# Work moved in front of a branch between two attention paths, and a row load issued one block ahead

## The reference, cut to what matters

```python
support = (inputs @ weight).reshape(-1, H, D).transpose(1, 0, 2)      # H = 4 heads, D = 64
f1 = einsum('hnd,hd->hn', support, weight_u)[:, None, :]              # s_j, by source node
f2 = einsum('hnd,hd->hn', support, weight_v)[:, :, None]              # s_i, by target node
masked = leaky_relu(f1 + f2, 0.2) * adj_mat
m = max over the row where masked != 0
e = where(mask, exp(masked - m), 0)
out = (e / e.sum(axis=2)) @ support + bias + inputs @ proj_w.T + proj_b
```

## Time and profile before

| | |
|---|---|
| median of 3 runs | 1848.31 us (1845.47, 1851.26, 1848.31) |
| profiled execution | 1845.97 us, span 1844.2 us |
| mean granted TensorE clock | 0.963 |
| TensorE busy | 1675.1 us, 91% of the span |
| VectorE busy | 929.3 us, 50% |
| ScalarE busy | 955.2 us, 52% |
| chain that ended last | TensorE 51%, VectorE 4%, DMA 2%, ScalarE 2%, issue 2% |

### The profile page before, as it was taken

One profiled execution on the slowest core, in us unless ns is written; L12 is line 12 of the kernel. 1 busy time (PEld: TensorE's weight loads), 2 busy tenths in 40 slices (PEclk: granted clock), 3 DMA queues, 4 the chain that ended last, 5 costly groups with the idle time before them and its releaser, 6 DMA issues.

```text
span 1844.2 us, 41619 instructions
## 1 busy us (share of the span) xinstructions
PE 1675.1 (91%) x13344; PEld 1547.9 (84%) x13345; DVE 929.3 (50%) x2185; ACT 955.2 (52%) x2192; POOL 350.6 (19%) x315
## 2 busy tenths in 40 slices
PE   4799999999799994767989989989988999999998
PEld 3588888778799994657989979989987999999997
DVE  4578877888322222338877868867773111111111
ACT  1143443543434432347989979979834443443443
POOL 2110000000266663210000000000001333333332
PEclk9899999999899997788999999999998999999999
DMA  9990000005388886200000000000094666666664
GB/s 159 107 164 10 9 9 17 29 18 200 114 208 206 207 212 174 80 14 7 17 15 13 14 13 18 9 18 18 3 332 157 178 189 174 179 190 173 181 187 94
DMA packets 85581, 189.95 MB, mean 103 GB/s; under 512 B 13209, under 2 KB 59545, under 8 KB 76665
## 3 DMA queue, kind: packets, MB, share of 16 engines
q1 hardware_dynamic: 51801, 138.33, 22.9%
q0 software_dynamic: 31504, 48.97, 16.7%
q10 hardware_dynamic: 2192, 1.58, 0.3%
HBM read 188.98 MB, written 33.11 MB: 120 GB/s over the span
## 4 chain that ended last, share of the span: by engine, by line
PE 51%; DVE 4%; DMA 2%; ACT 2%; issue 2%; ACTq 0%; DVEq 0%; POOL 0%; SPq 0%; POOLq 0%
PE bank L1625 23%; PE bank L2107 12%; PE bank L2146 11%; PE bank L619 1%; PE bank L616 1%; DMA arena<-proj_b 1%; ACT arena L1376 1%; PE bank L2114 1%; DMA arena<-qd 1%; DVE arena L1469 0%; DVE arena L1471 0%; PE bank L2036 0%; PE bank L2010 0%; PE bank L606 0%; DVE arena L1413 0%
## 5 line engine op out<-in xcount | busy, mean ns | idle before, releaser
L1625 PE MATMUL bank<-arena 128*128 128x195 bf16 x5408 | 475.9, 250 | 43.3 <-DVE arena L1471 35.7
L1625 PEld LDWEIGHTS bank<-arena 128*128 128x128 fp8e4 x5408 | 470.8, 98 | 48.5 <-issue 46.5
L1376 ACT ACTIVATE arena<-arena,m_row 128x512 fp8e5<-128x512 f32 (+1 forms) x672 | 401.6, 678 | 68.6 <-DVE arena L1471 46.0
L2107 PEld LDWEIGHTS bank<-X,arena 128*128 128x128 f32 x2832 | 337.0, 194 | 8.7 <-issue 2.6
L2107 PE MATMUL bank<-X,arena 128*128 128x128 f32 x2832 | 339.2, 277 | 0.1
L2210 DVE TENSOR_TENSOR arena<-bank,X 128x256 f32<-128x256 f32 x118 | 50.1, 425 | 562.3 <-PE bank L2146 508.9
L2146 PE MATMUL bank<-arena,X 128*128 x1416 | 325.0, 379 | 2.2 <-ACT X L2184 2.1
L1245 PE MATMUL bank<-arena 128*128 (+1 forms) x1352 | 312.1, 386 | 15.1 <-DVE arena L1151 15.0
L1245 PEld LDWEIGHTS bank<-arena 128*128 128x128 f32 x1352 | 252.5, 191 | 55.7 <-issue 20.9
L2146 PEld LDWEIGHTS bank<-arena,X 128*128 128x128 f32 x1416 | 259.9, 190 | 33.2 <-issue 2.6
L1103 ACT ACTIVATE bank<-arena,s_all 128x384 f32<-128x384 f32 (+1 forms) x234 | 133.7, 573 | 185.5 <-DVE arena L1143 182.9
(11 more groups left out here) (235 smaller groups left out, 1341.2 us busy)
## 6 DMA issues: line engine op xcount, KB each, us to landing
arena<-m1w SPq DMA_DIRECT2D x67, 1024.0 KB, 10.6
arena<-m0w SPq DMA_DIRECT2D x67, 512.0 KB, 6.9
xs<-X SPq DMA_DIRECT2D x4, 1664.0 KB, 7.0
arena<-qd SPq DMA_DIRECT2D x25, 256.0 KB, 3.3
arena<-adjT POOLq DMA_DIRECT2D x13, 448.0 KB, 12.7
arena<-adjT POOLq DMA_DIRECT2D x13, 384.0 KB, 10.8
xe<-zeros POOLq DMA_DIRECT2D x1, 3456.0 KB, 21.7
X<-x_in SPq DMA_DIRECT2D x2, 1664.0 KB, 11.3
```

Source lines behind the costliest of these rows:

```text
L1376: last = a.activation(self.sign[slot].bitcast(F8W)[:, q * W:q * W + nt * P], self.row[r][:, 0:nt * P], ACT.Sigmoid, scale=STEEP, bias=self ...
L1625: last = pe.matmul(bank[rb * NT + n][:, kind * KW:(kind + 1) * KW], self.split[slot][kind].bitcast(F8)[:, q * W + n * P:q * W + (n + 1) * ...
L2107: last = pe.matmul(bank[2 * s + c // 4][:, c % 4 * P:(c % 4 + 1) * P], self.W1[s][:, k * HID + c * P:k * HID + (c + 1) * P], self.rxt[s][: ...
```

## The change

Seen from each engine:

- **TensorE** runs `own_row_tensor` before `reach_tensor`.
- **SP** no longer waits for the store inside `own_row_sync`. The new `first_row_sync`, in front of the branch, waits for it and loads the row of head 0, block 0. `row_sync` is written out per head, with a loop over blocks inside, and issues the load of a block as the next one in order: blocks 1 to 6, then block 0 of the next head. The wait counts and buffers are those of before.
- **ScalarE** runs the new `early_scalar` in front of the branch: the two exponentials of s_j, the scaled copy, the exponential of `q_cols`, and a sigmoid of one column whose result isn't used.
- **VectorE** runs `early_vector` in place of `far_vector`: `q_cols`, the flag, and the first group of parts, interleaved, all in front of the branch. The row bound now goes to the third part of `q_cols` and not to `m_row`, which holds the scaled copy. The negated s_j (L642) moves to the far side, whose new opening is `far_begin_vector` and `far_begin_scalar`.

```diff
@@ reach_vector @@
-                if H > 1:
-                    v.tensor_scalar(neg_sj[:, 0:H * T], s_all[:, 0:H * T], -1.0, None, ALU.mult)
@@ far_vector: removed as a whole @@
@@ own_row_sync @@
                 sp.dma_start(qd[2 * HT:3 * HT, :], self.own).then_inc(self.own_stored, 16)
-                sp.wait_ge(self.own_stored, 16)
@@ row_sync @@
-                with sp.Fori(0, H) as h:
-                    def body(j, r, nt):
-                        sp.wait_ge(self.row_used[r], h * (4 - r) + j + 1)
-                        sp.dma_start(self.row[r][:, 0:nt * P],
-                                     flat[at(((2 * H + h) * T) * P + (2 * j + r) * self.W, nt * P)]
-                                     .partition_broadcast(P)).then_inc(self.row_loaded[r], 16)
-                    self.each_block(sp, body)
+                def load(h, k, r, nth, nt):
+                    sp.wait_ge(self.row_used[r], nth + 1)
+                    sp.dma_start(self.row[r][:, 0:nt * P],
+                                 flat[at(((2 * H + h) * T) * P + k * self.W, nt * P)]
+                                 .partition_broadcast(P)).then_inc(self.row_loaded[r], 16)
+                NT, half = self.NT, self.BLOCKS // 2
+                for h in range(H):
+                    with sp.Fori(0, half - 1) as j:
+                        load(h, 2 * j + 1, 1, 3 * h + j, NT)
+                        load(h, 2 * j + 2, 0, 4 * h + j + 1, NT)
+                    load(h, self.BLOCKS - 1, 1, 3 * h + half - 1, NT)
+                    load(h, self.BLOCKS, 0, 4 * h + half, NT // 2)
+                    if h + 1 < H:
+                        load(h + 1, 0, 0, 4 * (h + 1), NT)
+
+            def first_row_sync(self, sp):
+                H = self.H
+                sp.wait_ge(self.A.own_stored, 16)
+                sp.wait_ge(self.row_used[0], 1)
+                sp.dma_start(self.row[0], qd.rearrange("r p -> (r p)")[at(2 * H * T * P, self.W)]
+                             .partition_broadcast(P)).then_inc(self.row_loaded[0], 16)
+
+            def early_scalar(self, a):
+                H = self.H
+                for s in range(2):
+                    a.wait_ge(self.A.vp_free[s], PAIRS + 1)
+                a.activation(d_all[:, 0:H * T], s_all[:, 0:H * T], ACT.Exp, scale=SLOPE)
+                a.activation(self.exp_sj[:, 0:H * T], s_all[:, 0:H * T], ACT.Exp).then_inc(self.exp_ready, 1)
+                a.activation(self.steep_sj, s_all[:, 0:H * T], ACT.Copy, scale=STEEP).then_inc(self.steep_ready, 1)
+                a.wait_ge(self.row_steps, H + 3)
+                a.activation(q_cols[:, 0:2 * H * T], q_cols[:, 0:2 * H * T], ACT.Exp).then_inc(self.exp_ready, 1)
+                a.activation(rden[:, 0:1], s_all[:, 0:1], ACT.Sigmoid)
@@ sign_scalar: the four activations and the wait for row_steps removed from its head @@
@@ split_vector: its head, down to the first scale_group, becomes early_vector @@
+            def early_vector(self, v):
+                A, H = self.A, self.H
+                HT, st, fs = H * T, self.row_steps, A.far_steps
+                si, top, low = s_all[:, HT:2 * HT], q_cols[:, 2 * HT:3 * HT], found[:, 0:HT]
                 for h in range(H):
                     v.tensor_scalar(top[:, h * T:(h + 1) * T], ..., reach_all[:, h:h + 1], None, ALU.add).then_inc(st, 1)
+                v.tensor_reduce(far[:, :], reach_all[:, 0:2 * H], AXX, ALU.max).then_inc(fs, 1)
+                v.tensor_tensor(edges[:, 0:H], reach_all[:, 0:H], reach_all[:, H:2 * H], ALU.add).then_inc(fs, 1)
                 v.wait_ge(st, H)
                 v.scalar_tensor_tensor(out=low, in0=top, scalar=SLOPE, in1=top, ...).then_inc(st, 1)
+                v.wait_ge(fs, 2)
+                v.tensor_reduce(edges[:, H:H + 1], edges[:, 0:H], AXX, ALU.max).then_inc(fs, 1)
                 v.wait_ge(st, H + 1)
                 v.tensor_tensor(q_cols[:, 0:HT], si, low, ALU.subtract).then_inc(st, 1)
                 v.scalar_tensor_tensor(out=q_cols[:, HT:2 * HT], in0=si, scalar=SLOPE, in1=low, ...).then_inc(st, 1)
+                v.wait_ge(fs, 3)
+                v.scalar_tensor_tensor(out=far[:, :], in0=edges[:, H:H + 1], ..., in1=far[:, :], ...).then_inc(fs, 1)
+                v.wait_ge(fs, 4)
+                v.tensor_scalar(is_far[:, :], far[:, :], QUICK_REACH, None, ALU.is_ge).then_inc(A.far_known, 1)
+                v.wait_ge(self.exp_ready, 1)
+                self.scale_group(v, 0, 0, 4)
+                v.wait_ge(A.far_known, 1)
@@ first_block @@
                     self.scale_group(v, 1, 0, 4)
+                    v.wait_ge(self.exp_ready, 2)
@@ the block of the second layer @@
                 A1.own_row_sync(sp)
+                Q1.first_row_sync(sp)
                 sp.wait_ge(A1.far_known, 1)
...
                 A1.reach_vector(v)
-                A1.far_vector(v)
+                Q1.early_vector(v)
...
                 A1.own_row_scalar(a)
+                Q1.early_scalar(a)
                 a.wait_ge(A1.far_known, 1)
...
                 A1.values_tensor(pe)
+                A1.own_row_tensor(pe)
                 A1.reach_tensor(pe)
-                A1.own_row_tensor(pe)
```

More of the change, by code:

```diff
@@ L678, in bins_vector @@
                                     ALU.is_ge).then_inc(self.above_ready, 1)
[L680 to L693, removed]
             def own_row_tensor(self, pe):
@@ L1358, in sign_scalar @@
             def sign_scalar(self, a):
                 H, W = self.H, self.W
-                a.activation(d_all[:, 0:H * T], s_all[:, 0:H * T], ACT.Exp, scale=SLOPE)
-                a.activation(self.exp_sj[:, 0:H * T], s_all[:, 0:H * T], ACT.Exp).then_inc(self.exp_ready, 1)
-                a.wait_ge(self.row_steps, H + 3)
-                a.activation(q_cols[:, 0:2 * H * T], q_cols[:, 0:2 * H * T], ACT.Exp).then_inc(self.exp_ready, 1)
-                a.activation(self.steep_sj, s_all[:, 0:H * T], ACT.Copy, scale=STEEP).then_inc(self.steep_ready, 1)
@@ L1433, in scale_group @@
                 self.part_low(v, h, group, chunks)
-            def split_vector(self, v):
-                H, W, NT, HC = self.H, self.W, self.NT, self.HC
-                HT, st = H * T, self.row_steps
-                si, top, low = s_all[:, HT:2 * HT], m_row[:, 0:HT], found[:, 0:HT]
+            def early_vector(self, v):
+                A, H = self.A, self.H
+                HT, st, fs = H * T, self.row_steps, A.far_steps
+                si, top, low = s_all[:, HT:2 * HT], q_cols[:, 2 * HT:3 * HT], found[:, 0:HT]
                 for h in range(H):
@@ L1449, in split_vector, with far_begin_vector, far_begin_scalar @@
                                        op1=ALU.subtract).then_inc(st, 1)
-                v.wait_ge(self.exp_ready, 2)
-                self.scale_group(v, 0, 0, 4)
+                v.wait_ge(fs, 3)
+                v.scalar_tensor_tensor(out=far[:, :], in0=edges[:, H:H + 1], scalar=QUICK_REACH / QUICK_SPAN,
+                                       in1=far[:, :], op0=ALU.mult, op1=ALU.max).then_inc(fs, 1)
+                v.wait_ge(fs, 4)
[3 more added lines that the diff above has]
+                v.wait_ge(A.far_known, 1)
+            def far_begin_vector(self, v):
+                v.wait_ge(self.A.own_stored, 16)
+                v.wait_ge(self.row_loaded[0], 16)
+                v.wait_ge(self.exp_ready, 2)
+                v.wait_ge(self.steep_ready, 1)
+                v.tensor_scalar(neg_sj[:, 0:self.H * T], s_all[:, 0:self.H * T], -1.0, None, ALU.mult)
+            def far_begin_scalar(self, a):
+                a.wait_ge(self.row_loaded[0], 16)
+                a.wait_ge(self.parts_ready, 2)
+            def split_vector(self, v):
+                H, W, NT, HC = self.H, self.W, self.NT, self.HC
                 m32 = words(MASK_AT, MASK_WORDS).bitcast(U32)
@@ L2376, in _ @@
                 A1.reach_vector(v)
-                A1.far_vector(v)
+                Q1.early_vector(v)
                 with v.If(v.value_load(is_far[0:1, 0:1], min_val=0, max_val=1) > 0):
-                    v.wait_ge(A1.own_stored, 16)
+                    Q1.far_begin_vector(v)
                     A1.bins_vector(v)
@@ L2394, in _ @@
                 A1.own_row_scalar(a)
+                Q1.early_scalar(a)
                 a.wait_ge(A1.far_known, 1)
                 with a.If(a.value_load(is_far[0:1, 0:1], min_val=0, max_val=1) > 0):
+                    Q1.far_begin_scalar(a)
                     A1.count_scalar(a)
```

## The result

Over ten runs each, the changed kernel takes 1839.8 us in the median (1834.8 to 1846.5) and the kernel before 1847.3 us (1841.9 to 1851.3). The medians are 7.5 us apart. The ratio of the means is 0.9962, with a 95% interval of 0.9944 to 0.9979, so by it the change saves 7.0 us, between 3.9 and 10.3. The forecast was 5.4 us. A second set on another occasion gave 0.9964 (0.9951 to 0.9978): 6.6 us.

The account below looks back on a forecast made before the run. The prediction took a hand-over made of waits, ending at the first mask step, to bound the kernel there; 4.2 us at the start plus 1.2 between heads gave 5.4 us, so 1842.9 us (own range 1841 to 1845, wide 1839.5 to 1847.5).

Parts of the forecast that it names:

- Where the kernel was bound: Seam at 784 to 876 us: a hand-over made of waits, TensorE busy 6.05 of 20 us, no engine full.
- VectorE's chain: VectorE's work up to the first mask step: its start moves from 832.51 to 828.3, gaining 4.2 us (3.4 to 4.7).
- my lower start: Parts group on VectorE: begins after 1.75 us, at 821.55, if the flag's small instructions lie in the others' gaps.
- The last wait afterwards: Before the first mask step: VectorE's branch becomes the last wait, with ScalarE's signs ready some 1.1 us earlier.
- The second stall: VectorE's 1.77 us stand before L1448, after the branch: costed at 0, the other end being the whole 1.77.
- the stall at the branch: VectorE's 3.0 us with nothing to wait for after its branch, read as code of the taken side brought in.
- Loads at the head changes: Three row loads between heads, with constant addresses: 0.4 us each, all on the path, 1.2 us (bounds 0 and 1.5).
- My sign of being wrong: First mask step to end of attention: a longer stretch, or 3 us gaps at VectorE's loop, would refute the forecast.
- The slower rival: VectorE's loop over blocks loses its code, each jump back costing 3.0 us: 1850.9 us, chance 0.08.
- The sum: Whole kernel: 4.2 us at the start plus 1.2 between heads, 5.4 us or 0.29%, giving 1842.9 us.
- a change within 0.3%: Whole kernel: a difference under 5.5 us, counted as no change by a measurement, chance 0.56.
- the wide range: Whole kernel: 1839.5 to 1847.5 us, holding the first four cases with the median's spread, without the slow one.

Follow-up runs that it names:

- the second profile: The changed kernel run and profiled once more, nothing altered: ratio 0.9964 to the kernel before, first mask step at 10.00 us after the first reach reduction.
- 12 dead instructions: The kernel before with 12 never-executed VectorE instructions at the end of the far side: first mask step at 13.23 us and not 14.71.
- the short jump: The changed kernel without VectorE's part of the far side, so its branch skips some 3 instructions, not 271: ratio 0.9948, first mask step at 8.20 us.
- The early-table and row experiments: The changed kernel without the one-column sigmoid: first mask step 10.08 us; separately, with the first row load behind the branch: 11.24 us, ratio 0.9978.
- 116 dead instructions: The changed kernel with 116 never-executed VectorE instructions at the end of the far side: one stall of 5.46 us, first mask step at 12.39 us.
- The shift experiments: Never-executed VectorE instructions added: 12 to the kernel before (first mask step 13.23 us), 116 or 100 to the changed kernel (12.39 and 9.89 us).
- the alternating buffers: The changed kernel with two row buffers taking turns over all 28 blocks: 1824.75 us, ratio to the kernel before 0.9913.

## Why the prediction was right

**Where the kernel was bound, and VectorE's chain: right.** The start of the first mask step was the number to predict: 4.2 us gained forecast (3.4 to 4.7), 4.8 measured, 0.1 above that range, and 4.7 in the second profile. From the first parts instruction to the mask step it was 6.3 us, as forecast: the sequencer did go on under the last parts instruction, and the branch was through at 826.19, 0.07 us after that one ended. The term mis-sized is the one before it: from the four L1445 to the parts group it took 1.6 us against the 2.2 I took (my lower start had 1.75). Three of the flag's five small instructions cost nothing: L1456 starts 1.19 us after the first L1445, and where they aren't there and nothing stalls (12 dead instructions, L1441 to L1448) it is 1.18. The other two stand behind L1456, and the parts group starts 0.44 us after it.

**The last wait afterwards: right.** VectorE's branch and not ScalarE or the row. The slack forecast for ScalarE was 1.1 us; it was 1.7 (9.91 less the 8.20 of the short jump). The early-table and row experiments showed that 1.2 us more of table are just hidden and 3 us more of row load are not. Undoing VectorE's part alone undid the gain, although the interval (3.7 us faster to 2.0 slower) still holds the 1.8 us that the other parts should leave.

**The second stall: right here, by a wrong argument.** I costed it at 0 because the first mask step couldn't be reached by it and the parts would cover it. The code of the changed kernel stands where there is none. Where it does stand (116 dead instructions) it reaches the first mask step and nothing covers it: 2.4 us. That was a risk of 2.4 us that my range for the start didn't hold, and it went well by position. The shift experiments moved the first mask step by position alone, from 14.7 to 13.2 in one kernel and from 12.4 to 9.9 in the other. The Trainium skill's rule (Runtime: NRT & Kernel Launch, Instruction fetch mechanics), that code comes in blocks and a jump out of those held stalls, agrees with them; its block of 256 instructions they don't settle.

**TensorE's own entry: left out.** I read the stall at the branch as VectorE's alone. In the changed kernel TensorE's branch took 3.37 us (0.44 before), its sequencer stood another 3.1 us behind it, and the first product started 0.8 us later than its masks allowed. It cost nothing, since TensorE had caught up by its fourth step; that it did was not in the forecast.

**Loads at the head changes: the size right, the path wrong at one of three.** 0.4 each forecast, 0.44 measured each at the issue, alone as well as within the change; 1.3 us in all. I put all three on the path because TensorE stands there. At the second change it stands for its own jump, and its first product started 2.3 us after the masks allowed (2.0 in the kernel before), so by the row alone the gain is 0.9 us. With the loads written out alone, TensorE's three stands fell by 0.42, 0.37 and 0.48 us all the same; the 0.37 is the shorter branch, and it was luck for this term. What ScalarE waits also hangs on the landing, 3.0 to 4.3 us, which hides it in any one profile (0.6 us less in the first, 2.4 in the second). I had read rightly that the loads are not issued ahead at a head change: the alternating buffers prove it.

**My sign of being wrong was a bad one.** I had written that the forecast is wrong if the stretch from the first mask step to the end of the attention gets longer. In the first profile it did, by 0.6 us; in the second it was 2.3 us shorter. The products behind the stands took 0.9 us more in the first and 0.2 less in the second, which is as large as the term to be judged.

**The slower rival: did not come.** VectorE's loop branches took 50 to 63 ns as before:

```profile
L1623 DVEq COMPARE_BRANCH  x8: 50/56/63, 894.5 to 1305.1; - x8
```

**The sum.** 4.8 and 1.3 make 6.1 us by rows (5.7 without the second head change). The two timed comparisons say 7.0 (3.9 to 10.3) and 6.6 (4.1 to 9.0). They don't exclude either 5.4 or 6.1. I put the larger chance on a change within 0.3%; it came out at 0.38% and 0.36%, with intervals on both sides of that line. With the lower of my two starts for the parts group, which was the nearer one, the sum would have stood at 5.8, beyond the line. The absolute time was partly luck: 1839.8 lies 3.1 us under the 1842.9 forecast, below the forecast's own 1841 to 1845 and 0.3 us inside the wide range. Of the 3.1, 1.1 are the base, whose median over ten runs is 1847.3 and not the 1848.3 of three.

## What to carry to other kernels

Count a hand-over from an event that the change can't move, and not from the span: here the span's spread was as large as the gain. Work moved in front of a branch is worth what the one engine on the chain gains; the other moves only keep up with it, but some must (the row load), or they become the next wait. Before moving work, ask of a double buffer which two uses in order share a buffer: here a renumbering of buffers brought some 9 us on top of the change's 7. And a wait at a hand-over has to be checked on every engine that stands there: at one of three head changes it was TensorE's own jump that ended last.

## What the runs showed of the hardware that wasn't expected

**A jump's price goes by where the entered code stands.** VectorE stood 3.0 us at a jump over 271 instructions, nothing at a jump over 3, 3.0 at one over 371, and 5.5 at one over 387. The branch of TensorE's one jump back over its head loop took 3.3 to 4.9 us in the profiles, and its next product started another 3.6 to 4.0 us after that (kernel before, changed, alternating buffers). Written out, it is gone.

**A stand costs TensorE a second time, in clock.** These two windows are the first 5 us of products after the first head change, in the changed kernel (stand of 4.96 us) and in the one with alternating buffers (1.86 us). After the times come the length, five busy times with their counts, and then the granted clock, the figure before the DMA share:

```profile
965.30:970.30 5.00, 4.95 (x32) 4.58 (x33) 2.24 (x4) 5.00 (x9) 0.00 (x0) 0.53 0.00 0
```

```profile
960.10:965.10 5.00, 4.94 (x58) 4.97 (x59) 3.71 (x7) 5.00 (x9) 0.00 (x0) 1.00 0.00 0
```

After the longer stand the granted clock is 0.53, which is near the 1.2 GHz level, and TensorE does 32 products in 5 us. After the shorter one it is 1.00, the 2.4 GHz level, and it does 58. The stretch of 1296 products that follows took 113.2 us there and 111.0 here. Over all profiles it took 112.3 to 113.8 us after stands of 4.7 us or more, and 111.0 after stands under 2. So a long stand cost 1.3 to 2.8 us beyond its own length, and a longer one not always more: 112.3 us after 6.54, 113.8 after 5.62. Of the 15.6 us that alternating buffers took off the first profile of the changed kernel, 5.9 are such products and 8.1 the stands themselves. The 1.6 us in the first head aren't shown to be the edit's: the version with TensorE's loop written out has the same buffers and lacks them.

**A load with constant addresses is issued 0.44 us sooner** after the last sign, at 0.08 and not 0.52 us, than one whose addresses are worked out in registers behind the wait; it is 0.07 with nothing else changed.
